# A transformer block's second attention on one Trainium2 core: all Q/K pieces first, V woven with the maxima, and fewer, larger transfers

## The reference, cut to what matters

```python
x = x + 0.5 * _L0_ffn_ref(_layernorm(x), ...)
x = x + _L0_attn_ref(_layernorm(x), ...)
x = x + 0.5 * _L0_ffn_ref(_layernorm(x), ...)
x = x + 0.5 * _L1_ffn_ref(_layernorm(x), gate_w, w1, w2, w3)     # 8 experts, 2 of them for a token
x = x + _L1_attn_ref(_layernorm(x), wq, wk, wv, wo)              # the stage that the change is about
x = x + 0.5 * _L1_ffn_ref(_layernorm(x), gate_w, w1, w2, w3)

def attention_fwd(x, wq, wk, wv, wo, n_heads=32):                # 16 columns a head
    xq, xk, xv = ((x @ w.T).reshape(B, T, n_heads, hd) for w in (wq, wk, wv))
    xq, xk = rotary_pos_emb(xq), rotary_pos_emb(xk)              # pairs (even, odd), one angle for all: cos t, sin t
    scores = jnp.einsum('bqhd,bkhd->bhqk', xq, xk) * hd ** (-0.5)
    probs = softmax(where(causal, scores, NEG_INF))
    return jnp.einsum('bhqk,bkhd->bqhd', probs, xv).reshape(B, T, C) @ wo.T
```

## Time and profile before

| | us |
|---|---|
| median of 3 runs (1368.03 to 1370.95) | 1369.75 |
| the profiled execution, its own time | 1372.15 |
| its span, first to last instruction | 1370.4 |

### The profile page before, as it was taken

One profiled execution on the slowest core, in us unless ns is written; L12 is line 12 of the kernel. 1 busy time (PEld: TensorE's weight loads), 2 busy tenths in 40 slices (PEclk: granted clock), 3 DMA queues, 4 the chain that ended last, 5 costly groups with the idle time before them and its releaser, 6 DMA issues.

```text
span 1370.4 us, 26531 instructions
## 1 busy us (share of the span) xinstructions
PE 1185.6 (87%) x9782; PEld 486.0 (35%) x9782; DVE 866.3 (63%) x2491; ACT 350.0 (26%) x723; POOL 123.5 (9%) x151
## 2 busy tenths in 40 slices
PE   6799756999999994688789999999759889999982
PEld 3477422333333331333334444433323323333320
DVE  4731476767787763654888888841358657777753
ACT  4434420000000000121166666674100000000000
POOL 1100010111111100220100000000100111111100
PEclk9899887999999997799999999999869999999995
DMA  9000332047503244239514331005640533514545
GB/s 368 11 1 1 142 137 99 32 175 280 216 33 128 94 155 170 94 101 128 101 42 78 58 56 29 2 2 215 279 167 17 224 123 138 185 65 140 179 179 206
DMA packets 44521, 166.15 MB, mean 121 GB/s; under 512 B 7613, under 2 KB 14355, under 8 KB 40039
## 3 DMA queue, kind: packets, MB, share of 16 engines
q1 hardware_dynamic: 34415, 137.28, 30.3%
q0 software_dynamic: 5760, 18.88, 4.0%
q10 hardware_dynamic: 4216, 8.29, 2.7%
HBM read 786.00 MB, written 22.03 MB: 590 GB/s over the span
## 4 chain that ended last, share of the span: by engine, by line
PE 75%; DVE 12%; DMA 5%; issue 3%; ACT 3%; SPq 1%; POOL 1%; ACTq 0%; POOLq 0%; DVEq 0%
PE PS L954 28%; PE PS L972 13%; PE PS L1397 5%; PE PS L1360 4%; PE PS L1384 4%; DVE PS L1519 3%; PE PS L975 2%; PE PS L706 2%; PE PS L689 2%; PE PS L1424 2%; PE PS L1343 2%; PE PS L479 2%; PE PS L493 1%; DMA HH<-in_w 1%; PE PS L1348 1%
## 5 line engine op out<-in xcount | busy, mean ns | idle before, releaser
L954 PE MATMUL PS<-arena 128*32 128x400 f32 x3456 | 399.0, 504 | 8.0 <-DMA HH<-in_w 4.0
L954 PE MATMUL PS<-HH,arena 128*32 128x400 f32 x1152 | 398.5, 504 | 0.0
L1119 DVE STREAM_TRANSPOSE arena<-arena 32x128 f32<-32x128 f32 x544 | 164.7, 303 | 144.8 <-DMA arena<-h_scratch,RT 137.6
L954 PEld LDWEIGHTS PS<-arena 128*32 128x32 f32 x3456 | 141.4, 111 | 261.7 <-issue 257.2
L1519 DVE CUSTOM_DVE_ANT_0 PS<-PS,U 128x128 f32<-128x128 f32 (+7 forms) x256 | 188.0, 783 | 59.3 <-PE PS L1360 58.5
L1141 DVE STREAM_TRANSPOSE arena<-arena 32x192 f32<-32x192 f32 x576 | 211.4, 367 | 7.2
L972 PE MATMUL PS<-arena 128*32 128x512 f32 x1512 | 197.7, 604 | 15.0 <-DMA arena<-in_w2b 15.0
L1465 ACT ACTIVATE arena<-PS 128x512 f32<-128x512 f32 (+3 forms) x384 | 165.2, 496 | 74.0 <-PE PS L1387 48.4
L1001 ACT ACTIVATE arena<-PS 128x400 f32<-128x400 f32 x72 | 36.3, 504 | 363.4 <-PE PS L954 363.4
L954 PEld LDWEIGHTS PS<-HH,arena 128*32 128x32 f32 x1152 | 124.6, 111 | 0.0
L1360 PE MATMUL PS<-arena 96*128 96x512 bf16 (+3 forms) x384 | 104.0, 332 | 17.6 <-DVE arena L1519 13.7
(11 more groups left out here) (246 smaller groups left out, 1156.3 us busy)
## 6 DMA issues: line engine op xcount, KB each, us to landing
arena<-in_w SPq DMA_DIRECT2D x228, 1600.0 KB
arena<-in_w2a SPq DMA_DIRECT2D x114, 1536.0 KB
HH<-in_w SPq DMA_DIRECT2D x76, 1600.0 KB
HH<-in_w2a SPq DMA_DIRECT2D x38, 768.0 KB
arena<-in_w2a SPq DMA_DIRECT2D x38, 768.0 KB
arena<-in_w2b SPq DMA_DIRECT2D x152, 64.0 KB
arena<-split_scratch SPq DMA_DIRECT2D x72, 128.0 KB, 6.5
split_scratch<-arena SPq DMA_DIRECT2D x48, 128.0 KB, 2.3
```

The lines of the kernel that those rows point to most:

```text
L954: mm = eng.matmul(PS[SR * j:SR * j + SR, 2 * hf + m, 0:FH], XBT[:, u, c, SR * j:SR * j + SR], W13[j][:, c // 2, m, c % 2, hf * FH:(hf + 1) ...
L1119: tr = eng.transpose(XBT[SR * b:SR * b + SR, u, :, SR * a:SR * a + SR], src[:, :, SR * b:SR * b + SR])
```

## The change

It alters five things.

1. *Order.* `WORK` has all eight Q/K pieces first and the eight V tiles last. The head of the plan projects, rotates and splits the eight pieces; the V tiles are woven with the maxima, at positions -1.25 to 0.
2. *Two pieces ahead of the stage.* `pe_front_attn1`, at the end of the expert stage, does transposes 0 to 3, piece 0, transposes 4 and 5, piece 1, transposes 6 and 7. TensorE and ScalarE report the end of the stage before that and wait for it after.
3. *Weights.* Q's and K's weights land in `WRAW`; ScalarE copies them reordered into `WQKV` (16 copies), so that the stationary columns are contiguous and the projected rows come in the order of DRAM. The cosines are loaded behind the rows of y instead of at the start of the stage.
4. *Write-out.* A piece leaves in one transfer instead of six. So `s_pw` counts 16 for a piece.
5. *Restacking.* Group 0 is loaded alone, groups 1 to 3 together in 12 transfers of three times the length, and SP issues both Q's and K's. "ld 0" stands behind the split of piece 3, "ld 1" behind that of piece 5; the maxima of group 1 wait for the joint load.

```diff
-        WORK = [("qk", 1, 0, 0), ("qk", 1, 0, 1), ("qk", 0, 0, 0), ("qk", 0, 0, 1),
-                ("v", 0), ("v", 1), ("v", 2), ("v", 3), ("v", 4), ("v", 5), ("v", 6), ("v", 7),
-                ("qk", 1, 1, 0), ("qk", 1, 1, 1), ("qk", 0, 1, 0), ("qk", 0, 1, 1)]
+        WORK = [("qk", 1, 0, 0), ("qk", 0, 0, 0), ("qk", 1, 0, 1), ("qk", 0, 0, 1),
+                ("qk", 1, 1, 0), ("qk", 0, 1, 0), ("qk", 1, 1, 1), ("qk", 0, 1, 1),
+                ("v", 0), ("v", 1), ("v", 2), ("v", 3), ("v", 4), ("v", 5), ("v", 6), ("v", 7)]
...
-            for w in range(4):
+            for w in range(8):
                 plan += project(w) + [("rope", w)] + (split(w - 1) if w >= 1 else [])
-            plan += split(3)
-            for w in range(4, 12):
-                plan += project(w) + [("vc", w - 4)]
-                if 5 <= w < 9:
-                    plan.append(("ld", w - 5))
+                if w == 4:
+                    plan.append(("ld", 0))
+                if w == 6:
+                    plan.append(("ld", 1))
+            plan += split(7)
...
+            for w in range(8, 16):
+                at = (w - 8) * LEAD1 / 8 - LEAD1
+                others += [(at + LEAD1 / 8 * j / 4, u) for j, u in enumerate(project(w))]
+                others.append((at + LEAD1 / 8 * 0.99, ("vc", w - 8)))
...
+            rows = SPD[x][g // 4].rearrange("(a r) (f h) t -> a (r f) h t", r=2, f=HP)
+            n = 3 if g == 1 else 1
+            at = g % QRING
             for s in range(SLOTS):
-                rows = SPD[x][g // 4].rearrange("(a r) (f h) t -> a (r f) h t", r=2, f=HP)
-                eng.dma_start(dst[s * HD1:(s + 1) * HD1, g % QRING],
-                              rows[slots[s], :, (g % 4) * GH:(g % 4 + 1) * GH]).then_inc(S(f"s_ld{g % QRING}"), 16)
+                eng.dma_start(dst[s * HD1:(s + 1) * HD1, at:at + n].rearrange("p g h t -> p (g h) t"),
+                              rows[slots[s], :, at * GH:(at + n) * GH]).then_inc(S(f"s_ld{at}"), 16)
+        def restacked(g):
+            at = min(g, 1) if g < QRING else g % QRING
+            return S(f"s_ld{at}"), 32 * SLOTS * (1 if g < QRING or at >= 2 else 2)
...
+        def act_attn1_weights(eng):
+            eng.wait_ge(S("s_wraw"), 32)
+            for n in (1, 0):
+                for c in range(C):
+                    for half in range(2):
+                        cols2 = slice(half * 256, (half + 1) * 256)
+                        ins = eng.copy(WQKV[:, n, c, cols2].rearrange("p (two f h) -> p two f h", two=2, f=HP),
+                                       WRAW[:, n, c, cols2].rearrange("p (h f two) -> p two f h", f=HP, two=2))
+            ins.then_inc(S("s_wqk"), 1)
...
-                    for a in range(SLOTS):
-                        eng.dma_start(SPD[x][half, a, :, J * HT_:(J + 1) * HT_].rearrange("(f h) t -> h f t", f=HP),
-                                      PARTS[:, r % 2, a]).then_inc(S(f"s_pw{r % 2}"), 16)
+                    eng.dma_start(SPD[x][half, :, :, J * HT_:(J + 1) * HT_].rearrange("a p t -> p a t"),
+                                  PARTS[:, r % 2]).then_inc(S(f"s_pw{r % 2}"), 16)
...
+        EARLY1 = 2
+        def pe_front_attn1(eng, k):
+            for i in range(4):
+                pe_front(eng, k, i)
+            eng.wait_ge(S("s_wqk"), 1)
+            eng.wait_ge(S("s_wv"), 16)
+            eng.wait_ge(s_ht, NT * k + 4)
+            eng.wait_ge(S("m_yc"), NSTEP)
+            for w in range(EARLY1):
+                for j in range(2 * C):
+                    pe_project(eng, k, w, j)
+                pe_front(eng, k, 4 + 2 * w)
+                pe_front(eng, k, 5 + 2 * w)
...
-                    if g >= QRING:
-                        restack(eng, 0, g)
+                    restack(eng, 0, g)
...
-                elif kind == "ld" and u[1] < QRING:
-                    for b in range(2):
-                        eng.wait_ge(S(f"s_pw{b}"), 32 * SLOTS)
-                    restack(eng, 0, u[1])
```

More of the change, by code:

```diff
@@ L867, in sp_moe @@
                 rows_back(eng, i, 0)
+            if f == 0:
+                eng.wait_ge(S("s_csd"), 16)
+                eng.dma_start(CS.rearrange("p n t -> p (n t)"), CSD.broadcast_to([P, 2 * T])).then_inc(S("s_cs"), 16)
         def rows_back(eng, i, j):
@@ L984, in pe_moe @@
             if f == 0:
-                for i in range(NT):
-                    pe_front(eng, k + 1, i)
+                eng.drain().then_inc(stage_end, 1)
+                pe_front_attn1(eng, k + 1)
+                eng.wait_ge(stage_end, 4 * (k + 1))
         def act_moe(eng, link, k, f):
@@ L1293, in sp_attn1 @@
                     for b in range(2):
-                        eng.wait_ge(S(f"s_pw{b}"), 32 * SLOTS * (half + 1))
+                        eng.wait_ge(S(f"s_pw{b}"), 32 * (half + 1))
                     if g >= QRING:
@@ L1323, in pool_attn1, with pe_project @@
             pool_front(eng, link, k + 1)
+        def pe_project(eng, k, w, j):
+            at = 4 + 2 * (w % 2)
+            if j == 0 and w >= 2:
+                eng.wait_ge(S("s_rope"), done_before(w - 1, "qk"))
+                if done_before(w - 1, "v"):
+                    eng.wait_ge(S("s_vc"), done_before(w - 1, "v"))
+            if WORK[w][0] == "qk":
+                x, half, J = qk_of(w)
+                par, c = j // C, j % C
+                first = half * 256 + par * P
+                mm = eng.matmul(PS[:, at + par, :], WQKV[:, x, c, first:first + P], HS[k][1][:, c, J * HT_:(J + 1) * HT_],
+                                start=(c == 0), stop=(c == C - 1))
+                last = j == 2 * C - 1
+            else:
+                i = WORK[w][1]
+                mm = eng.matmul(PS[:, at, :], HS[k][1][:, j, i * P:(i + 1) * P], WQKV[:, 2, j, :],
+                                start=(j == 0), stop=(j == C - 1))
+                last = j == C - 1
+            if last:
+                mm.then_inc(S("s_proj"), 1)
+        EARLY1 = 2
[11 more added lines that the diff above has]
+                pe_front(eng, k, 5 + 2 * w)
         def pe_attn1(eng, k):
-            eng.wait_ge(S("s_wqkv"), 48)
             eng.wait_ge(s_ht, NT * k + NT)
@@ L1332, in pe_attn1 @@
                 if kind == "pm":
[L1333 to L1352 removed]
+                    if u[1] >= EARLY1:
+                        pe_project(eng, k, *u[1:])
                 elif kind == "max":
@@ L1356, in pe_attn1 @@
                     if h == 0 and i == 0:
-                        eng.wait_ge(S(f"s_ld{slot}"), 16 * 2 * SLOTS * (g // QRING + 1))
+                        eng.wait_ge(*restacked(g))
                     for lo in range(0, wide, HT_):
@@ L1596, in _ @@
                     act_attn1(act, link, k)
-                end_stage(act, k)
+                if not (kind == "moe" and instance(k) == 0):
+                    end_stage(act, k)
         @block.vector
@@ L1625, in _ @@
                     pe_attn1(pe, k)
-                end_stage(pe, k)
+                if not (kind == "moe" and instance(k) == 0):
+                    end_stage(pe, k)
 def laid_out(x):
```

38 lines of the change are left out of this document (8 added, 30 removed).

## The result

| | us |
|---|---|
| before, 20 runs beside it | 1370.99 (1366.66 to 1380.07) |
| after, 20 runs | 1363.09 (1357.43 to 1373.40) |
| ratio after to before | 0.9947, 95% interval 0.9928 to 0.9966 |
| the profiled execution after, its own time | 1363.76 |
| its span | 1361.9 |

A forecast was written before the change was run, and what follows sets the result against it. TensorE's order of work from the first exponent matmul on is unchanged, so that matmul's start sets the time: 682.4 against 686.58, 4.2 us sooner. The median 1369.75 less 4.2 gives 1365.5 us; range 1357 to 1374.

The forecast's parts named there:

- Early pieces at the low clock: Piece 0 starts at 565.4, 4.3 us sooner, about 3.5 us of it at 1.2 GHz, and takes 8.7 us.
- VectorE's chain: Rotating and splitting costs VectorE 7.16 us a piece; unless transfers hold it, it reaches the maxima at 637.3, 4.4 later.
- The write-out behind the restacking: Piece 4's write-out queues behind group 0's load until 634; ScalarE waits, so VectorE reaches the maxima at 642.4.
- The joint load: Groups 1 to 3 together, 4.72 MB at 133 GB/s from 635.5, take 35.5 us and land at 672.5.
- rival C: Load lands between 674.5 and 679, first exponent matmul at 683 to 688; total 1367 to 1372 us, unchanged; chance 0.21.
- The weave: V work woven with group 0's maxima: 39 us, TensorE setting the pace, 1.7 for a low clock; ends at 681.4.
- The last link: Transfers of the turned maxima land 6.3 us after L1367 starts, at 682.4, and release the first exponent matmul.
- The sum: First exponent matmul at 682.4 against 686.58, 4.2 us sooner, so 1365.5 us for the whole kernel.
- The rule weighed for the load: A transfer gets only ports its partitions reach: 109 GB/s for 16 partitions, load landing at 680, total 1372.
- A: Restacking queue no worse: pieces 4 and 5 leave beside the loads, or longer rows go faster; 1360.5 us; chance 0.18.
- B: Joint load late, at 116 GB/s, landing at 681.7; first exponent matmul at 690.5, 3.9 us later; 1373.7 us; chance 0.18.

The follow-up runs named there:

- after, again: The kernel after the change, with nothing altered, timed and profiled a second time: 1363.01 us, ratio to before 0.9947 (0.9918 to 0.9975).

## Why the prediction was right, point by point

The sign, the place and the mechanism were right. The prediction's clock was that of the profile of before; 555.95 is taken off here.

| step | predicted | after | after, again |
|---|---|---|---|
| piece 0 starts | 9.5 | 9.7 | 9.7 |
| piece 0 takes | 8.7 | 8.84 | 9.85 |
| last piece ends | 69.7 | 69.4 | 70.4 |
| VectorE reaches the maxima | 86.5 | 83.1 | 84.5 |
| joint load lands | 116.6 | 115.9 | 118.6 |
| from first maxima to first exponent matmul | 40.0 | 41.5 | 42.8 |
| first exponent matmul | 126.5 | 124.6 | 127.3 |

- *Early pieces at the low clock.* Held. That VectorE's chain takes up what they win is what the prediction said, and the timed run without them shows no loss beyond its interval.
- *VectorE's chain.* The pace of 7.16 us a piece held: the last rotation starts at 623.43, 70.9 us in (predicted 70.7).
- *The write-out behind the restacking.* Piece 4 was held as said, and ScalarE waited. Its size was too large: VectorE reached the maxima 3.4 and 2.0 us sooner than predicted. Two terms did it. A piece's own write-out was taken as 4.7 us, between bounds of 3 and 7, and it is 3.5. The larger is what piece 4 needs behind group 0's load: 4 us were taken (630 to 634), but it landed 1.5 us behind that load in the first profile and 1.9 in the second. So piece 4's transfer landed at 618.12 + 9.43 = 627.55, 75 us in, where 634 (78) was predicted. From there to the maxima it took 8.1 us, for 8.4.
- *The joint load.* 133 GB/s from 79.6 us on was predicted. Counted from when piece 5 had left, at 78.0 and 79.2, it took 37.9 and 39.4 us, which is 125 and 120 GB/s. An earlier start and a lower rate cancel to within 2 us, which is luck. The landing is the least certain term, as the rivals said: with 118.6 it lies at the edge of rival C. What the prediction missed is that the rate depends on the form of the load. It named that as a thing that would make it wrong, and had no row for it.
- *The weave.* 1.5 to 2.8 us longer than predicted. The low clock behind TensorE's idleness cost more than the 1.7 us of loss allowed for. These are the windows after (PEclk is third from the end):

```profile
630.00:640.00 10.00, 3.56 (x7) 1.53 (x8) 6.54 (x14) 3.58 (x4) 0.00 (x0) 0.50 1.03 125
640.00:645.00 5.00, 4.90 (x14) 1.69 (x12) 3.11 (x7) 0.18 (x1) 0.00 (x0) 0.91 1.05 128
```

  From 635.65 to 640 it was half and then 0.91 for 5 us, a loss of 4.35 / 2 + 0.45 = 2.6. In the repeat, 2.46 us of waiting for the load come on top.
- *The last link.* The prediction let the transfers of the turned maxima come last, 1.0 us behind the end of TensorE's own work. In both profiles the row of the first exponent matmul names ScalarE's last copy of V instead, after 0.25 us; TensorE's work before it ended at 676.12 + 0.79 = 676.91. The distance from L1409 to that matmul, 6.15 us, is still close to the 6.3 predicted.
- *The sum.* The first exponent matmul came 6.1 and 3.3 us sooner than before by the two profiles, 4.7 in the mean, for 4.2 predicted. That this is so close is partly luck: VectorE's start was put 2.0 to 3.4 us too late, the weave 1.5 to 2.8 too short. Timed, the gain is 7.3 us, 4.7 to 9.9, and in the second measurement 7.3 of 3.4 to 11.2. What the stage does not account for, some 2.6 us, lies within the intervals and within the scatter of code that did not change: from the first exponent matmul to the end it is 683.8 us before, and 684.8 and 683.2 after. Ahead of the stage the two profiles are 3.4 and 5.2 us shorter than the one of before. The old order's is 3.9 shorter there too (552.02), and its time was not less than before's, so this is not read as a gain; with one profile of before it stays open.
- *Slips that change nothing.* The second wait for a V copy stands behind the fourth V tile, so behind tile 3 where the first stands behind tile 1. By the prediction's own working C ends at 1371, not 1372.

The rule weighed for the load fares as follows. The window of 640 to 650 us in the kernel after shows 117 GB/s, the one from 632 to 667 in the repeat 113. The Trainium skill (SBUF — State Buffer, section Door 1: The DMA port swizzle) ties a transfer to the ports that its partitions reach, an estimate of 109 GB/s for 16 partitions; the long rows come near it. The 36 short loads, each into 16 partitions too, ran at 174 and 199, so it is no bound on a row of transfers that reach different partitions. No run here tells whether overlap of neighbouring transfers is the reason.

Of the rivals, A was half right: piece 4 left nearly beside the loads, and VectorE's start, 639.0 on the prediction's clock, lies between A's 637.3 and the 642.4 of the sum. But ScalarE did wait for piece 4, and the longer rows did not go faster. B did not come. C is what the second profile is near.

## What to carry to other kernels

When work is moved between two phases, ask which engine the phase was long for: here the weave shrank by 12 us because VectorE's rotations and splits left it (46.5 us of work became 32.0), where TensorE's work in it fell by 4.7 us only. Two limits that end within a few microseconds of each other have to be lifted together; each lifted alone can show little, and the one left may even make it worse by letting the clock fall, as the profile with the woven splits alone suggests. A load that several consumers share should not be one transfer with one semaphore if the first consumer needs a third of it, and a single profile cannot judge an effect smaller than the scatter of the clock and of the transfers.

## What the runs showed of the hardware

- Rows three times as long were slower, not faster: 12 transfers of 384 KB into 16 partitions each went at 113 to 140 GB/s, 36 of 128 KB at 174 and 199, from one queue, with the same total. The 48 short loads of the old order went at 150 from one queue (window of 615 to 650 us), and at 124 to 135 from two before the change; why was not tried.
- The same joint load took 34.0 to 42.3 us from its last issue to its landing in eight profiles of five kernels.
- In one profile the granted clock fell to 0.50 in a wait of 3.48 us between dense matmuls. In another it stayed at 1.00 through two waits of 3.77 and 2.82 us close together.
- A 768 KB write-out over 128 partitions in a single transfer took SP 0.36 to 0.42 us to issue. It landed 3.5 us later where no load stood ahead of it in the queue, and 9.4 behind twelve loads of 128 KB.
